# A graph-network kernel: the scores, softmax and edge stages of an attention layer joined into one pipelined stage of four chunks, and three of four heads weighed by ScalarE

## The reference

```python
def _gat(x, ei_src, ei_dst, W, a_src, a_dst, b, heads, out_ch, concat):
    ...
    h = (x @ W).reshape(n, heads, out_ch)
    al_s = jnp.einsum('nhc,hc->nh', h, a_src)
    al_d = jnp.einsum('nhc,hc->nh', h, a_dst)
    e = jax.nn.leaky_relu(al_s[src] + al_d[dst], 0.2)
    emax = jax.ops.segment_max(e, dst, num_segments=n)
    ee = jnp.exp(e - emax[dst])
    denom = jax.ops.segment_sum(ee, dst, num_segments=n)
    alpha = ee / (denom[dst] + 1e-16)
    out = jax.ops.segment_sum(h[src] * alpha[:, :, None], dst, num_segments=n)
    ...
```

## Time and profile before

| what | us |
|---|---|
| median of 3 runs (5494.01 to 5509.8) | 5496.4 |
| the profiled execution, its own time | 5452.6 |
| its span, from first to last instruction | 5450.9 |
| layer 1, scores to end of edge loop | 1873.2 to 2769.8 |
| layer 2, the same | 2922.5 to 3817.8 |
| layer 3, the same | 3936.0 to 4731.9 |
| mean granted clock of TensorE (share of 2.4 GHz) | 0.819 |

### The profile page before, as it was taken

How to read it: one execution, slowest core, us unless ns; L and a number is a source line. 1 busy time by engine, 2 the same in 40 slices (tenths; PEclk the granted TensorE clock), 3 DMA queues, 4 the chain that set the end, 5 groups by cost and what they waited for, 6 DMA issues and landing times. The chain is left out here.

```text
span 5450.9 us, 85101 instructions
## 1 busy us (share of the span) xinstructions
PE 3889.5 (71%) x22668; PEld 3121.2 (57%) x22669; DVE 2871.4 (53%) x6524; ACT 1797.9 (33%) x5670; POOL 2234.9 (41%) x2473
## 2 busy tenths in 40 slices
PE   5577776887997684777778667777664443667996
PEld 3455555686886474656546656556563322456885
DVE  4577777432002696555567955555784443662112
ACT  0566675221221224444422254444230000021221
POOL 0656663002221025666611356666037777502221
PEclk9788888988998767888888678888856665778998
DMA  2666663004556464666634556665373333304555
GB/s 80 180 180 180 187 186 106 17 25 153 181 185 156 129 172 130 182 183 182 183 114 133 155 149 184 181 181 166 109 215 91 91 91 94 89 29 160 185 182 168
DMA packets 348485, 782.46 MB, mean 144 GB/s; under 512 B 52869, under 2 KB 156908, under 8 KB 339692
## 3 DMA queue, kind: packets, MB, share of 16 engines
q0 software_dynamic: 145920, 459.41, 29.5%
q1 hardware_dynamic: 202348, 320.55, 18.8%
HBM read 729.52 MB, written 50.26 MB: 143 GB/s over the span
## 5 line engine op out<-in xcount | busy, mean ns | idle before, releaser
L1827 POOL DMA_INDIRECT h<-h_table,src_of x1392 | 1420.3, 1020 | 665.8 <-issue 387.6
L1816 PE MATMUL ps<-h,gat_edges_work 128*128 128x261 f32 x3712 | 978.9, 428 | 381.8 <-DVE h L1928 259.4
L1816 PEld LDWEIGHTS ps<-h,gat_edges_work 128*128 128x128 f32 x3712 | 782.1, 214 | 578.4 <-DVE h L1928 205.9
L1937 DVE TENSOR_TENSOR acc<-acc,ps 128x522 f32 (+1 forms) x696 | 418.4, 601 | 919.0 <-remote 596.7
L1850 ACT ACTIVATE h<-h,gat_shared 128x128 f32<-128x128 f32 x1856 | 592.7, 390 | 655.5 <-DMA h<-h_table,src_of 637.2
L724 POOL DMA_INDIRECT edges_rows<-kv_table,src_of x464 | 456.3, 983 | 415.5 <-DVE edges_out_rows L823 160.6
L1816 PE MATMUL ps<-h,gat_edges_hot 128*128 128x259 f32 x928 | 314.9, 495 | 344.1 <-DVE h L1928 179.3
L1928 DVE TENSOR_TENSOR h<-h,gat_shared 128x512 f32<-128x512 f32 x696 | 481.3, 693 | 38.3 <-DMA h<-h_table,src_of 37.2
L1816 PEld LDWEIGHTS ps<-h,gat_edges_hot 128*128 128x128 f32 x928 | 204.7, 240 | 453.9 <-DVE h L1928 168.8
L1325 DVE TENSOR_TENSOR moe_experts_result<-ps,moe_experts_b 128x512 f32<-128x512 f32 x64 | 44.3, 692 | 788.9 <-PE ps L929 788.9
L918 PE MATMUL ps<-moe_experts_turned,moe_experts_w 128*128 128x256 f32 x2048 | 455.9, 381 | 0.0
(11 more groups left out here) (349 smaller groups left out, 5709.8 us busy)
## 6 DMA issues: line engine op xcount, KB each, us to landing
moe_experts_w<-in_L_ffn_W SPq DMA_DIRECT2D x128, 1024.0 KB
gat_scores_rows<-src_rows SPq DMA_DIRECT2D x174, 256.0 KB, 3.8
gat_scores_rows<-dst_rows SPq DMA_DIRECT2D x174, 256.0 KB, 4.4
h<-h_table,src_of POOLq DMA_INDIRECT x1392
edges_dst_row<-dst_rows SPq DMA_DIRECT2D x58, 256.0 KB
h_table<-h SPq DMA_DIRECT2D x10, 1280.0 KB
h<-h_table SPq DMA_DIRECT2D x10, 1280.0 KB
h<-picked_out SPq DMA_DIRECT2D x48, 256.0 KB, 3.7
```

The costliest lines, as they stand in the source:

```text
L1816: mm = nc.tensor.matmul(k.ps[t % S * 2 + q][:, 0:PIECE], hot[:, t // BATCH % 3, t % BATCH * 2 + e, :], g.rows[:, t % RING, e, q * PIECE:(q ...
L1827: nc.gpsimd.indirect_dma_start(g.rows[:, r, e, 0:W], None, g.table, bass.IndirectOffsetOnAxis(ap=k.src_of[:, 2 * t + e:2 * t + e + 1], axis=0)
L1937: v.tensor_tensor(acc, acc, k.psum[:, t % S * 2:t % S * 2 + PIECES, 0:PIECE], ALU.add).then_inc(added, 1)
```

## The change

`phase_gat_scores` and `phase_gat_edges` become one stage, `phase_gat_layer`, written out on every engine. The items are cut into four chunks of 64 (the last has 40). Before item 0 there is a prologue: the 32 pairs of chunk 0 are scored (steps -64 to -33), then its softmax is done in 20 steps. After that the loop over items carries, inside the items of chunk c, the scores of chunk c+1 (in three of every four items, from the chunk's first to its 42nd) and its softmax (one of 20 steps at each of items 44 to 63 of the chunk). So 84 pairs and three softmaxes lie inside the loop. Because a destination can have edges in two chunks, the forward maximum is carried over, and the sums of the one tile in question are rescaled at each chunk's border (`rescale`).

Other parts of it:

- Of four heads VectorE weighs one, ScalarE three (`by_dve = 1`). In layer 3, with one head, VectorE weighs it as before.
- TensorE sums an item as one piece of 512 columns, and the other 9 columns as small matmuls of their own into a PSUM bank that four items share. VectorE adds them item by item, each with a register load (`add_tails`). Layer 3 has no such tail, and its PSUM ring is six deep (S = 6, LAG = 5).
- The copy of destination scores out of PSUM moves from ScalarE to VectorE; both `choose` copies of a pair are ScalarE's, none GpSimd's.
- Edge-index rows have two buffers in place of four; the one-hot matrices of scores three in place of four; PSUM banks for scores two in place of four.
- ScalarE clears `acc` before its first `choose`, since `acc` no longer serves as scratch for the scores.
- GpSimd's gathers start with the stage, in the prologue.

```diff
-        for t in range(ITEMS):
-                for q in range(PIECES):
-                    for e in range(2):
-                        mm = nc.tensor.matmul(k.ps[t % S * 2 + q][:, 0:PIECE], hot[:, t // BATCH % 3, t % BATCH * 2 + e, :],
-                                              g.rows[:, t % RING, e, q * PIECE:(q + 1) * PIECE], start=(e == 0), stop=(e == 1))
+    by_dve = 1
+    by_act = H - by_dve
+
+    def scored(t):
+
+        if t < 0:
+            c, j = 0, t + CH
+        else:
+            c, j = t // CH + 1, (3 * (t % CH) + 2) // 4 if t % 4 < 3 else CH
+        q = c * CH // 2 + j
+        return q if 0 <= j < CH // 2 and q < PAIRED else None
+
+    def softmax_step(t):
+
+        c, n = (0, t + CH // 2 - 1) if t < 0 else (t // CH + 1, t % CH - CH + 20)
+        return (c, n) if c < CHUNKS and 0 <= n < 20 else (c, None)
...
+                for e in range(2):
+                    mm = nc.tensor.matmul(k.ps[t % S][:, 0:MAIN], hot[:, t // BATCH % HOTS, t % BATCH * 2 + e, :],
+                                          g.rows[:, t % RING, e, 0:MAIN], start=(e == 0), stop=(e == 1))
+                if TAIL:
+                    for e in range(2):
+                        mm = nc.tensor.matmul(k.ps[S + t // BATCH % 2][:, t % BATCH * TAIL:(t % BATCH + 1) * TAIL],
+                                              hot[:, t // BATCH % HOTS, t % BATCH * 2 + e, :],
+                                              g.rows[:, t % RING, e, MAIN:FULL], start=(e == 0), stop=(e == 1))
...
+            pe.wait_ge(cut, 1)
+            for t in range(-CH, ITEMS):
+                if t >= 0:
+                    sum_item(t)
+                q = scored(t)
+                if q is not None:
+                    products(q)
+                c, n = softmax_step(t)
+                if n is not None:
+                    softmax(c, n)
...
+            act.copy(k.acc[:, :, 0:FULL], nought[:].rearrange("p (t a) -> p t a", t=1).to_broadcast([P, TILES, FULL])).then_inc(cleared, 1)
+            for t in range(-CH - 2, ITEMS):
+                q = scored(t + 2)
+                if q is not None:
+                    choose(q)
+                if t >= 0:
+                    scale(t)
+                c, n = softmax_step(t)
+                if n is not None:
+                    softmax(c, n)
...
+            for t in range(-CH - 2, ITEMS + LAG):
+                if 0 <= t < ITEMS:
                     weigh(t)
+                q = scored(t + 2)
+                if q is not None:
+                    one_hots(q)
+                q = scored(t - 2)
+                if q is not None:
+                    take_scores(q)
+                c, n = softmax_step(t)
+                if n is not None:
+                    softmax(c, n)
                 if t >= LAG:
                     add(t - LAG)
+                    if TAIL and (t - LAG) % BATCH == BATCH - 1:
+                        add_tails((t - LAG) // BATCH)
```

More of the change, by code:

```diff
@@ L1643, in _ @@
         @block.sync
         def _(sp):
-            def load(b, slot):
+            for b in range(ITEMS // 4):
+                if b >= NB:
+                    sp.wait_ge(lo_hots, 2 * (b - NB) + 2)
                 for j, table in enumerate((k.src_rows, k.dst_rows)):
-                    sp.dma_start(rows[:, j, slot, :], item_rows(table, 4 * b, 4)).then_inc(row_in[slot], 16)
-            for slot in range(BATCHES):
-                load(slot, slot)
-            turns, over = divmod(ITEMS // 4 - BATCHES, BATCHES)
@@ L1652, in _ @@
-            with sp.Fori(0, turns) as i:
-                for slot in range(BATCHES):
-                    sp.wait_ge(hots, i * RING + ((slot + 1) * 4 // G + 4))
-                    load(i * BATCHES + (BATCHES + slot), slot)
-            for slot in range(over):
-                sp.wait_ge(hots, turns * RING + (slot + 1) * 4 // G + 4)
-                load(turns * BATCHES + BATCHES + slot, slot)
-        def tables(n):
-            return parts[:].rearrange("p c (h t) -> p c h t", t=TILES)[:, :, :, bass.ds(n, 1)].rearrange("p c h a -> p c (h a)")
@@ L1839, in _, with tables, choose @@
-            act.wait_ge(exped, 1)
-            act.wait_ge(tailed, 1)
-            for t in range(ITEMS):
+            def tables(n):
+                return parts[:].rearrange("p c (h t) -> p c h t", t=TILES)[:, :, :, bass.ds(n, 1)].rearrange("p c h a -> p c (h a)")
+            def choose(q):
+                if q >= 4:
+                    act.wait_ge(made, q - 3)
+                for j in range(2):
+                    n = act.value_load(k.item_tile[0:1, 2 * q + j:2 * q + j + 1], min_val=0, max_val=TILES - 1)
+                    last = act.copy(of_item[:, q % 4, j, :, :], tables(n))
+                last.then_inc(chosen, 1)
@@ L1853, in _ @@
         @block.vector
         def _(dve):
[L1855 removed]
+            v, c_, cc = nc.vector, Chain(dve, link), Chain(dve, cut_link)
             v.memset(nought[:], 0.0).then_inc(noughts, 1)
[L1858 to L1864 removed]
@@ L1874, in _ @@
-            for h in range(H):
-                for b in range(BLK):
-                    c.mark(v.scalar_tensor_tensor(run[:, h, b, :], s.head[:, b, :], cin[:, b, h:h + 1], run[:, h, b, :],
-                                                  ALU.add, ALU.max))
-            c.wait()
-            for h in range(H):
-                c.mark(v.tensor_tensor_scan(flat(back[:, h])[:, ::-1], flat(s.next[:])[:, ::-1], flat(run[:, h])[:, ::-1], -BIG,
-                                            ALU.add, ALU.max))
```

495 lines of the change are left out of this document (265 added, 230 removed).

## The result

| | us | ratio to before |
|---|---|---|
| before, 4 runs | 5503.1 (5494.01 to 5516.62) | |
| after, 4 runs | 5618.1 (5607.56 to 5623.04) | 1.0204, 95% [1.0176, 1.0233] |
| profiled execution of after, its span | 5607.6, 5605.8 | |

The change makes the kernel 2% slower on this chip. I had forecast 5366 us, and a range that ended at 5566: wrong in direction and outside the range. Profiled executions differ by 155 us (5452.6 to 5607.6), of which 144.6 lie in the three layers: 896.6, 895.3 and 795.9 us became 974.3, 976.7 and 781.4. That is more than the change's own share: the profiled execution of before was 41 us shorter than the shortest run in the table.

What follows compares the result with a forecast made beforehand. Gathers were taken to pace the edge loop, and VectorE to hold up the two stages before it. Layers of 861, 861 and 738 us save 36 + 36 + 58 = 130 us, giving 5366 us, range 5226 to 5566.

Steps and rivals of the forecast that it cites:

- The prologue: Stage ahead of the loop's first item: 92 us in layers 1 and 2, 74 in layer 3, not hidden.
- A pair takes 1.49 us now: Prologue of layers 1 and 2: with the copy out of PSUM a pair takes 1.64 us, 32 pairs 53 us.
- The row buffers: Layer 3's prologue: two buffers give four pairs in about 6 us, 1.5 us a pair, 48 us.
- 38 late sums: Edge loop before the change: VectorE's add waits 4.8 us on average, unexplained; a ring of 12 items hides most.
- The gathers of 12 items fill the ring meanwhile: Prologue: GpSimd's gathers run beside it, with no time of their own in its 92 us.
- Items with scores: Loop of layers 1 and 2: 110 items at 3.5 us, 385 us, with TensorE's 3.2 us the largest engine sum.
- the ratio 0.72: Busy share of the fullest engine in the first graph layer's loop; at it, items with scores would take 4.4 us.
- rival 2: Loop: VectorE bounds, every late sum counts; scored items 4.1 us, +107 us, 5603; decides past 3.58 us mean; chance 0.22.
- Softmax items: Loop of layers 1 and 2: 60 items at 3.4 us, 2.8 with hand-overs plus late sums, 204 us.
- layer 3's loop: Layer 3: GpSimd stays the bound at 2.5 us, the loop keeps 2.85 us an item, 661 us.
- The clear: Prologue, ahead of ScalarE's first choose: 11.1 us in layers 1 and 2, 5.6 in layer 3.
- The rule against the change: Items with scores: one-hots block GpSimd's descriptor writes, at most 0.36 us an item, 2.9 in place of 2.53 us.

Runs made afterwards that it cites:

- c1: The kernel before, unchanged, run again on another chip of the slower kind: ratio 0.9989 to before, loops of 666 us.
- e1: The changed kernel with VectorE taking a pair's scores one step after the products in place of two, faster kind of chip: ratio 1.0117 to before.
- e4: The changed kernel with VectorE weighing two of four heads in place of one, faster kind of chip: ratio 1.0088 to before.
- c4: The changed kernel with gathers paced by pairs' products, scores taken one step after products in the prologue alone, clear beside the first softmax, slower kind: ratio 0.9998 to before.
- e13: The changed kernel without VectorE's nine-column adds and their register loads, TensorE's narrow matmuls kept, slower kind of chip: ratio 0.9891 to before.
- e7: The changed kernel with the ring's gathers for item t waiting for the products of t pairs, faster kind of chip: ratio 0.9917 to before.
- e14: The changed kernel with two 261-column pieces, paced gathers, sooner prologue takes, later clear, and VectorE weighing two of four heads, slower kind: ratio 0.9671 to before.
- e11: The changed kernel with sums in two pieces of 261 columns, no separate tails and a PSUM ring of three, slower kind: ratio 0.9806 to before.
- e3: The changed kernel with ScalarE's clear moved after the prologue's last choose, beside the softmax, faster kind of chip: ratio 0.9904 to before.
- e6: The kernel before with only the split changed, VectorE weighing one of four heads and ScalarE three, slower kind: ratio 1.0000 to before.
- e12: The changed kernel with two 261-column pieces, paced gathers, scores taken one step after products in the prologue, and the later clear, slower kind: ratio 0.9598 to before.
- c3: The changed kernel, unchanged, as control on the slower kind of chip: ratio 1.0226 to before.

## Why the prediction failed

Its layers (861, 861 and 738 us) came to 974.3, 976.7 and 781.4: 272 us more, in the pieces below. Some of that is no step of the prediction: the layers of the unchanged kernel take some 31 us more in c1 than in the trace from which I forecast.

1. **The prologue, wrong in two steps: 162 us** (49.7 + 49.3 + 62.9). Its first 13 us (2 + 11) and its softmax (22) were right: the first product starts 13.5 us in, and from pair 31 to the first item are 21.9. The 57 us between for 32 pairs took 106. The step "A pair takes 1.49 us now ... it gains the copy out of PSUM ... 32 x 1.64 = 53" took VectorE's work for the pace, although the change itself has fewer buffers and fixed distances. The row buffers, to which I gave the limit in layer 3, weren't it in layer 1. The pace was the round of hand-overs, from three one-hot buffers, two PSUM banks and scores taken two steps late; e1 tests the distance, and no run changed the buffers. 30 x (2.82 - 1.64) is 35 us; e1 takes 25 of it back. Late reports are the second step: 19 us in layer 1 (141.7 against e4's 122.6) and 50 in layer 3 (136.9 against 86.7). The two come to 54 in layer 1, 5 more than the miss, since the 4 us for filling and emptying were too many. My text had looked at 38 late sums in the earlier trace rows, called them inexplicable, and said in the same breath that a stage with a ring hides them. "The gathers of 12 items fill the ring meanwhile" was costed at nothing; c4 shows that on this kind of chip just that was dear.
2. **Items with scores, 82 us** (38 + 44). 3.5 was "nearer to the sum" than to the ratio 0.72 of the earlier trace rows. TensorE's total of 3.2 us was right (137.3/43 = 3.2), in part by luck: its sums took 2.82 us, where I had 2.26, a pair's products 0.85 ((22.2 + 14.4)/43), where I had 0.92, and the two overlap. VectorE was 2.6 busy, and TensorE, the fullest engine, is busy 0.83 of the time. Most of what stands above the largest sum is VectorE's chain of adds, which I had sized nearly right (0.5 us, 0.67 found) but put only into its own sum of 2.96: three quarters of it isn't busy time, and another engine's larger sum didn't cover it. While VectorE stands in four waits of its own, it weighs nothing for TensorE; e13 shows 0.43 us an item for the adds. The kind of chip has a share too: with nothing late the same items take 3.46 us (e7), and no run shows what makes the 0.37 between. My rival 2 had VectorE as the pace, which e4 and e14 bear out, and was nearer in size (4.1), with the point of 3.58 for the mean item. The loop's mean was 832.6/232 = 3.59, just at it; the prologue did the rest.
3. **Softmax items, 41 us**: 3.75 and 3.74 for 3.4. Without the separate tails they are 3.42 (e11), without VectorE's nine-column adds 3.47 (e13). So the tails cost 0.3 us here, less than the 0.5 in my sum, and the step that failed lies in the rest, the 0.5 for hand-overs and 0.6 for late sums: without tails my sum would have been 2.9. No run parts those two.
4. **The plain items** lost 5 and 2 us, drain included, and **layer 3's loop** gained 19 (forecast 664, 644.6 found: 2.78 us an item, 0.04 from its old 2.82). That its mean held is luck in part: its items took 3.1 us with scores and 1.86 in the last chunk, not one pace, and the same groups of items in the unchanged kernel from 1.5 to 3.2.
5. **The clear** stood where I had put it, but moving it gave 3 us of 11 on the faster kind, since the third pair then waits for its row load (e3). Before, the clear ran beside that load.
6. **The rule against the change** didn't bite: 84 gathers beside 30 one-hots took 0.980 us each, against 0.988 in the earlier trace rows. In the whole trace the 98 gathers beside whose start (0.1 us before to 0.6 after) a one-hot begins have a median of 1.00 us, the others 0.95. The Trainium skill, "SBUF — State Buffer", section "SBUF: two separate sides", has GpSimd's descriptor writing wait for a two-port `tensor_scalar`; these rows show at most 0.05 us a gather, where a one-hot lasts 0.48.

The two parts of the title fared differently. Three and one is a gain, but only in the joined stage: 43 us a layer in e4, 33 in e14, none in e6. Joining as such gains too once its two private costs, the prologue's round and the separate tails, are gone: with the old split it stands at 0.9671 (e14), with three and one at 0.9598 (e12), where the changed kernel is at 1.0226.

On the tails, what the rows show first: a nine-column float32 matmul has a record of 252 ns against 694 for 512 columns, and its weight load takes 219 ns. The Trainium skill, "TensorE: Matmul & The Clock Gate", section "LDWEIGHTS (loading the stationary operand)", gives a load's time by the columns of the weights; what is then multiplied has no part in it. The trace agrees on that: in the same stretch the loads take 219 ns in front of nine columns and 207 in front of 512. It shows too that the type counts, since loads of 128 bfloat16 columns take 104 ns there (L1744).

## What to carry to other kernels

When stages are joined, sum each engine's work, but also write down the round of waits that a buffer count and the order of steps on one engine make, and its length; where that round is the only work, as in a prologue, it is the pace. A distance between steps that is right inside a loop can be wrong ahead of it, and the reverse. Don't split a few columns off an accumulation when two equal pieces fit: small adds with a register load each, in a chain, cost their latency four times over, and here no other engine's larger sum covered that idle time. A wait that a trace shows and can't explain belongs in the price of whatever new stage meets the same conditions.

## What the chips showed that I had not expected

The first graph layer's loop is the same code in all kernels. Here are the longest waits of ScalarE there (200 to 900 us) on the slower kind (c3), then on the faster (e7), and the window of e7, to be read against the earlier trace rows, which are of the slower kind:

```profile
ACT edges_out_rows L748 <- remote: 159.6, 39, 12.2
```

```profile
ACT edges_out_rows L748 <- DVE edges_score L817: 77.5, 68, 2.3
```

```profile
200.00:900.00 700.00, 565.34 (x2128) 381.58 (x2128) 563.35 (x1329) 495.56 (x1360) 423.78 (x428) 0.95 0.61 184
```

On the slower kind 39 waits end with a "remote" event, up to 12.2 us; on the faster the view has none of that sort at all. The DMA moves 181 GB/s on the one and 184 on the other, so it isn't short of bandwidth. On the faster kind plain items took 2.14 us in place of 2.6, items with scores 3.46 in place of 3.82. In the kernel before's loop on the slower kind three sums are reported within 0.2 us of each other (c1, 2310.71 to 2310.90), where TensorE needs 1.76 us for one: what is late there is the report. And each of VectorE's four small adds in a row has 0.50 us of idle time ahead of 0.17 of work.
